# Splitting two of seven key tiles of the attention scores into hi and lo products, with the split made on ScalarE and GpSimd

## What is computed

```python
def _L0_xattn_ref(query, ref, Wq, bq, Wk, bk, Wv, bv):
    Q = query @ Wq + bq
    K = ref @ Wk + bk
    V = ref @ Wv + bv
    scores = jnp.einsum('bqh,bkh->bqk', Q, K)
    attn = jax.nn.softmax(scores, axis=-1) * norm_fact
    return jnp.einsum('bqk,bkh->bqh', attn, V)

x = x + _L0_xattn_ref(_layernorm(x), ctx_1024, Wq, bq, Wk, bk, Wv, bv)
x = x + _L0_attn_ref(_layernorm(x), ...)
x = x + _L0_ffn_ref(_layernorm(x), ...)
```

## Time and profile before

| | before |
|---|---|
| time, median of 3 runs | 238.4 us (237.71 to 238.56) |
| time of the profiled execution | 238.81 us |
| its span, first to last instruction | 237.0 us |
| TensorE busy (matmuls) | 224.4 us, 95% |
| VectorE, ScalarE busy | 136.1 us, 136.6 us |
| GpSimd busy | 105.0 us, 44% |
| granted TensorE clock, mean | 1.000 |
| loaded from HBM | 52.56 MB |

### The profile page before, as it was taken

The page is one execution under the profiler, slowest core; times in us unless marked ns, Lnnn a source line. Parts: engine busy times, 40 slices in busy tenths (PEclk is TensorE's granted clock), DMA queues, the critical chain, the costliest instruction groups (busy, mean ns, idle before and its releaser), DMA issues.

```text
span 237.0 us, 4100 instructions
## 1 busy us (share of the span) xinstructions
PE 224.4 (95%) x1513; PEld 188.8 (80%) x1513; DVE 136.1 (57%) x321; ACT 136.6 (58%) x252; POOL 105.0 (44%) x64
## 2 busy tenths in 40 slices
PE   7989999999999989789998999999999999999994
PEld 7746777777777767579985889974689999999994
DVE  2237555555555554623877876516144748977784
ACT  5146666655555557326878666726405848766570
POOL 1065566666666667330579960000000536555450
PEclk9999999999999999999999999999999999999999
DMA  6999999999999991799700000000000585980000
GB/s 181 376 426 414 417 417 415 420 417 416 423 416 408 410 421 70 247 431 420 319 0 4 0 0 3 1 0 3 0 0 3 178 314 203 408 314 7 0 3 22
DMA packets 8531, 52.92 MB, mean 223 GB/s; under 512 B 953, under 2 KB 1218, under 8 KB 6466
## 3 DMA queue, kind: packets, MB, share of 16 engines
q1 hardware_dynamic: 8514, 52.69, 55.7%
HBM read 52.56 MB, written 0.13 MB: 222 GB/s over the span
## 4 chain that ended last, share of the span: by engine, by line
PE 82%; DMA 6%; DVE 5%; ACT 2%; issue 1%; SPq 1%; ACTq 0%; DVEq 0%
PE psum L427 37%; PE psum L495 14%; PE psum L724 8%; PE psum L422 7%; DMA late_sb<-in_ctx_T 6%; PE psum L622 3%; PE psum L614 3%; PE psum L418 2%; PE psum L648 2%; PE psum L675 1%; PE psum L557 1%; DVE w_lo L1284 1%; PE psum L572 1%; PE psum L631 1%; PE psum L567 1%
## 5 line engine op out<-in xcount | busy, mean ns | idle before, releaser
L360 POOL TENSOR_TENSOR ctx_lo<-ring,ctx_hi 128x1792 fp32r<-128x1792 f32 x13 | 52.4, 4034 | 40.3 <-ACT ctx_hi L788 40.3
L410 POOL TENSOR_TENSOR h_lo<-ring,h_hi 128x512 fp32r<-128x512 f32 x16 | 24.8, 1548 | 66.6 <-ACT h_hi L963 60.6
L427 PE MATMUL psum<-late_sb,work 128*128 128x448 f32 x112 | 44.7, 542 | 1.4 <-DMA late_sb<-in_ctx_T 1.4
L427 PEld LDWEIGHTS psum<-late_sb,work 128*128 128x128 f32 x112 | 20.2, 190 | 18.2 <-issue 17.7
L795 ACT ACTIVATE probsT_hi<-psum 128x512 fp32r<-128x512 f32 (+1 forms) x28 | 13.7, 541 | 32.0 <-PE psum L422 32.0
L1023 DVE TENSOR_REDUCE smalls<-psum 128x1 f32<-128x896 f32 x14 | 15.3, 1091 | 23.3 <-PE psum L427 23.3
L427 PE MATMUL psum<-xT,late_sb 128*128 128x128 f32 x224 | 26.2, 276 | 0.1
L427 PEld LDWEIGHTS psum<-xT,late_sb 128*128 128x128 f32 x224 | 25.5, 192 | 0.3 <-DVE xT L1254 0.3
L788 ACT ACTIVATE ctx_hi<-ring 128x1792 fp32r<-128x1792 f32 x13 | 22.1, 1698 | 2.9 <-DMA ring<-in_ctx 2.9
L495 PE MATMUL psum<-ctx_hi,probsT_hi 128*128 128x256 f32 x98 | 20.6, 327 | 2.5 <-DVE probsT_lo L1047 2.5
L1047 DVE TENSOR_TENSOR probsT_lo<-psum,probsT_hi 128x512 fp32r<-128x512 f32 (+1 forms) x28 | 16.2, 619 | 7.4 <-ACT probsT_hi L795 7.4
(11 more groups left out here) (230 smaller groups left out, 415.0 us busy)
## 6 DMA issues: line engine op xcount, KB each, us to landing
late_sb<-in_ctx_T SPq DMA_DIRECT2D x14, 896.0 KB, 13.7
ring<-in_ctx SPq DMA_DIRECT2D x14, 896.0 KB, 12.2
late_sb<-in_late SPq DMA_DIRECT2D x10, 825.0 KB, 12.1
late_sb<-in_experts SPq DMA_DIRECT2D x8, 1024.0 KB, 6.1
late_slots<-in_experts SPq DMA_DIRECT2D x8, 1024.0 KB, 7.8
early_sb<-in_early SPq DMA_DIRECT2D x1, 512.0 KB, 3.6
early_sb<-in_early SPq DMA_DIRECT2D x1, 465.0 KB, 17.7
work<-in_levels SPq DMA_DIRECT2D x1, 416.0 KB, 19.4
```

The lines of the kernel that those rows point to most:

```text
L360: nc.gpsimd.tensor_tensor(ctxNv[1][:, r % 2], ring[:, r], ctxNv[0][:, r % 2], ALU.subtract).then_inc(s["ctx_lo"], 1)
L410: nc.gpsimd.tensor_tensor(hT[1][:, e % 2, at, :], h32[:, at, :], hT[0][:, e % 2, at, :], ALU.subtract).then_inc(s["h_lo_done"], 1)
L427: last = nc.tensor.matmul(o, lhs(c), rhs(c), start=(c == 0), stop=(c == n - 1))
```

## The change

The scores of groups 3 to 13 are no longer wholly fp32. Of a group's seven key tiles the first two (SPLIT = 256 columns) are computed as three fp32r products: G_hi x T_hi, G_lo x T_hi and G_hi x T_lo, two chunks each, six matmuls of 256 columns. The other five tiles stay fp32, as 448 columns in one bank and 192 in the other.

G_hi is made once by ScalarE and G_lo once by VectorE. T_hi (a 128x512 rounding of the transposed context) is made for each group by ScalarE, ahead of the probs_hi copies, and T_lo (a 128x512 subtraction) by GpSimd. Both are double-buffered. These tiles lie where the last five parts of the late weights go, so these five loads now wait for the last scores. TensorE's part of the loop is unrolled.

```diff
         E_sb = sb("early_sb", EARLY_N)
+        with ExitStack() as overlay:
+            overlay.enter_context(nc.sbuf_tensor("first_parts", [P, FIRST_PARTS * PART_N], F32))
+            T_parts = [overlay.enter_context(nc.sbuf_tensor(f"ctxT_{part}", [P, 2 * DC * SPLIT], F32R)) for part in ("hi", "lo")]
+            G_parts = [overlay.enter_context(nc.sbuf_tensor(f"G_{part}", [P, D], F32R)) for part in ("hi", "lo")]
         W_sb = sb("late_sb", LATE_N + W_SLOTS * EXPERT_N)
...
+            sp.wait_ge(s["scores_ready"], NG)
             for i in range(FIRST_PARTS, LATE_PARTS):
                 part(i, "late2_in")
-            sp.wait_ge(s["scores_ready"], NG)
...
+            def ctxT_lo_parts(g, r):
+
+                pool.wait_ge(s["T_hi"], g - 2)
+                nc.gpsimd.tensor_tensor(Tv[1][:, r % 2], ringT[:, r, :, 0:SPLIT], Tv[0][:, r % 2], ALU.subtract).then_inc(s["T_lo"], 1)
+
+            ctx_lo_parts(0, 0)
+            ctx_lo_parts(1, 1)
+            with pool.Fori(0, 2) as i:
                 for j in range(RING):
-                    ctx_lo_parts(i * RING + j, j)
...
+                    ctx_lo_parts(i * RING + (j + 2), (j + 2) % RING)
+                    ctxT_lo_parts(i * RING + (j + 3), (j + 3) % RING)
+            for g in range(2 * RING, NG - 3):
+                ctx_lo_parts(g + 2, (g + 2) % RING)
+                ctxT_lo_parts(g + 3, (g + 3) % RING)
...
-                for hf in range(2):
-                    last = wide(bank[2 * (r % 2) + hf][:, 0:HALF], lambda c: G[:, c * P:(c + 1) * P],
-                                lambda c: ringT[:, r, c, hf * HALF:(hf + 1) * HALF])
+                b = 2 * (r % 2)
+                last = wide(bank[b + 1][:, 0:HALF], lambda c: G[:, c * P:(c + 1) * P], lambda c: ringT[:, r, c, HALF:GK])
+                plain = SPLIT if split else 0
+                last = wide(bank[b][:, plain:HALF], lambda c: G[:, c * P:(c + 1) * P], lambda c: ringT[:, r, c, plain:HALF])
+                if split:
+                    pe.wait_ge(s["T_hi"], g - 2)
+                    terms = [(u, v, c) for u, v in ((0, 0), (1, 0), (0, 1)) for c in range(DC)]
+                    for i, (u, v, c) in enumerate(terms):
+                        if i == 2 * DC:
+                            pe.wait_ge(s["T_lo"], g - 2)
+                        last = nc.tensor.matmul(bank[b][:, 0:SPLIT], half(G_parts[u], c), Tv[v][:, r % 2, c, :],
+                                                start=(i == 0), stop=(i == len(terms) - 1))
...
-            with pe.Fori(0, 2) as i:
-                for j in range(RING):
-                    r = (j + 2) % RING
-                    scores(i * RING + (j + 2), r, i * 16 + (32 if j >= 2 else 16))
-                    attend(i * RING + j, j)
-                    probs_transposes(i * RING + (j + 1))
-            for g in range(2 * RING, NG - 3):
+            scores(2, 2, 16, split=False)
+            attend(0, 0)
+            probs_transposes(1)
+            pe.wait_ge(s["g_done"], 4)
+            for g in range(1, NG - 3):
                 scores(g + 2, (g + 2) % RING, 16 * ((g + 2) // RING + 1))
                 attend(g, g % RING)
                 probs_transposes(g + 1)
...
+            def ctxT_hi_parts(g, r, filled):
+
+                act.wait_ge(ctxT_in[r], filled)
+                act.wait_ge(s["scores_ready"], g - 1)
+                nc.scalar.activation(Tv[0][:, r % 2], ringT[:, r, :, 0:SPLIT], ACT.Copy).then_inc(s["T_hi"], 1)
+
             with act.Fori(0, 2) as i:
                 for j in range(RING):
                     exps(i * RING + (j + 1), (j + 1) % RING)
+                    ctxT_hi_parts(i * RING + (j + 3), (j + 3) % RING, i * 16 + (32 if j >= 1 else 16))
                     probs_hi_parts(i * RING + (j + 1))
```

More of the change, by code:

```diff
@@ L15 @@
 HALF = GK // 2
+SPLIT = 2 * P
 HK, HV = 4, 8
@@ L144, in perceiver @@
         ctxNv = [part[:, :].rearrange("p (b t d) -> p b t d", b=2, d=D) for part in ctxN]
+        Tv = [part[:, :].rearrange("p (b c k) -> p b c k", b=2, c=DC) for part in T_parts]
         probsT = [part[:, :].rearrange("p (t q) -> p t q", q=T) for part in PT]
@@ L200, in perceiver @@
             late2_in wqk_in dve_chain act_chain pool_chain conv_v y_free mx_done l_done out_ready x_ident aq_done al_low al_middle al_high kn_done xc_done
-            var_done ln_sd ln_xn ln_T ln_xT q_ready q_done q_done_dve g_ready g_done g_done_act qb_ready qb_done bv_ready
-            ctx_hi ctx_lo last_hi last_lo probsT_hi scores_ready max_ready exp_done alpha_done probs_transposed probsT_lo pv_done acc_done
+            var_done ln_sd ln_xn ln_T ln_xT q_ready q_done q_done_dve g_ready g_done qb_ready qb_done bv_ready
+            T_hi T_lo ctx_hi ctx_lo last_parts probsT_hi scores_ready max_ready exp_done alpha_done probs_transposed probsT_lo pv_done acc_done
             o_T o_copied att_ready
@@ L360, in ctx_lo_parts @@
                 nc.gpsimd.tensor_tensor(ctxNv[1][:, r % 2], ring[:, r], ctxNv[0][:, r % 2], ALU.subtract).then_inc(s["ctx_lo"], 1)
-            with pool.Fori(0, 3) as i:
-                for j in range(RING):
-                    ctx_lo_parts(i * RING + j, j)
-            for g in range(3 * RING, NG - 1):
-                ctx_lo_parts(g, g % RING)
+            def ctxT_lo_parts(g, r):
[4 more added lines that the diff above has]
+            with pool.Fori(0, 2) as i:
+                for j in range(RING):
+                    ctx_lo_parts(i * RING + (j + 2), (j + 2) % RING)
[3 more added lines that the diff above has]
+                ctxT_lo_parts(g + 3, (g + 3) % RING)
             g, at = NG - 1, slice(0, 4)
@@ L464, in _, with scores @@
             nc.tensor.matmul(bank[3][:, 0:D], sixteenth[:, :], bv_sb[:, :], start=True, stop=True).then_inc(s["bv_ready"], 1)
-            def scores(g, r, filled, first=False):
+            def scores(g, r, filled, first=False, split=True):
                 if not first:
@@ L493, in attend @@
                         if last_group:
-                            pe.wait_ge(s["last_lo"], 1)
+                            pe.wait_ge(s["last_parts"], 2)
                     last = nc.tensor.matmul(bank[6 + r % 2][:, 0:D], probsT[a][:, t, :], ctxNv[b][:, r % 2, t, :],
@@ L497, in attend @@
                 last.then_inc(s["pv_done"], 1)
-            pe.wait_ge(s["g_done"], 1)
-            pe.wait_ge(s["g_done_act"], 1)
-            scores(0, 0, 16, first=True)
+            pe.wait_ge(s["g_done"], 2)
+            scores(0, 0, 16, first=True, split=False)
             pe.wait_ge(s["qb_done"], 2)
-            scores(1, 1, 16, first=True)
+            scores(1, 1, 16, first=True, split=False)
             probs_transposes(0, first=True)
-            with pe.Fori(0, 2) as i:
-                for j in range(RING):
-                    r = (j + 2) % RING
-                    scores(i * RING + (j + 2), r, i * 16 + (32 if j >= 2 else 16))
-                    attend(i * RING + j, j)
-                    probs_transposes(i * RING + (j + 1))
-            for g in range(2 * RING, NG - 3):
+            scores(2, 2, 16, split=False)
[3 more added lines that the diff above has]
+            for g in range(1, NG - 3):
                 scores(g + 2, (g + 2) % RING, 16 * ((g + 2) // RING + 1))
@@ L768, in _ @@
             act.wait_ge(s["g_ready"], 1)
[L769 removed]
+            nc.scalar.activation(G[:, 0:P], bank[6][:, 0:P], ACT.Copy).then_inc(s["g_done"], 1)
             def exps(g, r, first=False):
@@ L801, in _ @@
             ctx_hi_parts(1, 1, 16, first=True)
+            act.wait_ge(s["g_done"], 2)
+            nc.scalar.activation(G_parts[0][:, :], G, ACT.Copy).then_inc(s["g_done"], 1)
+            def ctxT_hi_parts(g, r, filled):
+                act.wait_ge(ctxT_in[r], filled)
+                act.wait_ge(s["scores_ready"], g - 1)
+                nc.scalar.activation(Tv[0][:, r % 2], ringT[:, r, :, 0:SPLIT], ACT.Copy).then_inc(s["T_hi"], 1)
             with act.Fori(0, 2) as i:
@@ L808, in _ @@
                 exps(g + 1, (g + 1) % RING)
+                ctxT_hi_parts(g + 3, (g + 3) % RING, 16 * ((g + 3) // RING + 1))
                 probs_hi_parts(g + 1)
@@ L1053, in _ @@
             probs_lo_parts(0)
+            dve.wait_ge(s["g_done"], 3)
+            V.tensor_tensor(G_parts[1][:, :], G, G_parts[0][:, :], ALU.subtract).then_inc(s["g_done"], 1)
             with dve.Fori(0, 2) as i:
@@ L1071, in _ @@
             dve.wait_ge(s["pv_done"], g - 1)
-            V.tensor_copy(ctxNv[0][:, g % 2, at], ring[:, g % RING, at]).then_inc(s["last_hi"], 1)
+            V.tensor_copy(ctxNv[0][:, g % 2, at], ring[:, g % RING, at]).then_inc(s["last_parts"], 1)
             maxima(g, g % RING)
             accumulate(g - 1, (g - 1) % 2)
-            dve.wait_ge(s["last_hi"], 1)
-            V.tensor_tensor(ctxNv[1][:, g % 2, at], ring[:, g % RING, at], ctxNv[0][:, g % 2, at], ALU.subtract).then_inc(s["last_lo"], 1)
+            dve.wait_ge(s["last_parts"], 1)
```

(1 more changed line is left out.)

## The result

| | before | after |
|---|---|---|
| time, median | 238.32 us | **312.29 us** (310.98 to 313.35) |
| ratio to before | | 1.3106 (95% interval 1.3048 to 1.3164) |
| profiled execution, span | 238.81, 237.0 us | 312.66, 310.7 us |
| mean granted TensorE clock | 1.000 | 0.889 |

The kernel is 74 us slower. The forecast was 306 us, the range 288 to 320.

A forecast was written before the change was run, and what follows sets the result against it. TensorE, busy 95% of the span and 82% of the chain, was taken to bound the kernel. 238.8 + 50.8 (queue chain) + 0.3 (group 13) = 289.9 us; +16 for the clock gives 306 us, range 288 to 320.

The forecast's parts named there:

- Part 1: TensorE's split score blocks: 2.88 us against 3.01, 0.13 us less each, 1.4 us in all over eleven blocks.
- Part 2: ScalarE's T_hi: a 0.63 us copy once a step, hidden in 2.55 us of idle time; copies of G cost nothing.
- Part 3: GpSimd's T_lo behind ctx_lo closes a chain inside one step: 11.37 us against 6.29, 289.9 us at full clock.
- Part 4: TensorE's clock falls in each 5.2 us wait: 1.6 us a step, bounds 0 to 3.4, +16 us, giving 306.
- all of the path at the low clock: Rival, 13%: in the loop TensorE's clock isn't back before the transposes are done, 3.4 us a step, 324 us.
- no cost: Rival, 20%: the queue chain holds, but TensorE's clock stays or is back before T_lo arrives, 289.9 us.
- Part 5: Five late weight loads wait for the last scores; 10 us of loading, first read over 60 us later: costs nothing.
- The rival on the other side: Rival, 4%: no new chain on GpSimd, T_lo in hand by TensorE's fifth product; only 1.4 us gained, 237.4 us.
- the signs given ahead: Profile after: steps of 11 to 14.5 us, ten TensorE waits of about 5, GpSimd-led chain, PEclk below 9 in loop.

The follow-up runs named there:

- last version: The change with T_lo ahead of ctx_lo, 448 product columns (T_lo's second chunk on VectorE), group 13 fp32, G_hi and G_lo made right after G: 236.10 us.
- bank versions: The change with T_lo ahead of ctx_lo and 448 product columns; G_lo on VectorE 238.45 us, or on GpSimd with group 13 fp32 237.06 us.
- 38-dummy run: The change with 38 dummy 64x64 matmuls on TensorE between its fourth product and the wait for T_lo: 295.27 us, ratio 1.2379.
- first bank version: The change with T_lo ahead of ctx_lo, 448 instead of 256 columns as products, T_lo's second chunk on VectorE: 238.45 us, ratio 0.9976.

## Why the prediction was right, point by point

**Part 1, TensorE's own work: right.** 0.15 us a block (6.13 against 6.29) where 0.13 was worked out. In the change it was worth nothing, as said.

**Part 2, ScalarE: right, with one price wrong off the path.** T_hi takes 0.63 us and is hidden; the run without T_lo loses nothing to it. But of G_lo I said "at most some 0.6 us". It took 4.07 us:

```profile
19.82 4.04 POOL L366 TENSOR_TENSOR ctx_lo<-ring,ctx_hi 128x1792 fp32r<-128x1792 f32 x1 [2.92 <-ACT ctx_hi L809]
...
20.08 4.07 DVE L1086 TENSOR_TENSOR G_lo<-work,G_hi 128x256 fp32r<-128x256 f32 x1 [0.44 <-ACT G_hi L824]
```

It began while GpSimd was in ctx_lo of group 1, which ended at 23.86; G_lo ended at 24.15. VectorE reads two SBUF tiles in it, as in L1284 of the earlier trace rows. I had used the Trainium skill's rule ("SBUF — State Buffer", section "Who interferes with whom") for GpSimd's price and not for VectorE's, where it was the larger by far: 4.07 us, where the same subtraction takes 0.42 in the last version, at 10.08 us, with GpSimd idle. In the change it cost nothing, since TensorE reached its first split block at 24.20 us, when G_lo was just done. In the bank versions G_lo came 2 us late, on VectorE as on GpSimd, until it was made early.

**Part 3, the queue: right, with some luck in the last digit.** The step at full clock was forecast at 11.37 us; the 38-dummy run has 11.41. ctx_lo took 3.97 us for the 4.04, T_lo 1.26 for the 1.30, the hand-over to TensorE 0.04 for the 0.14, together some 0.25 us less than forecast; the two products took 0.50 after a wait at full clock, for the 0.24 of the sum, which is as much more. The errors cancel. The wait was 5.0 us for the forecast 5.2. Group 13 waited too, for the eleventh of the eleven waits. By its own terms 289.9 us, by experiment 291.4.

**Part 4, the clock: the mechanism right, the size too small.** This is the term that was off: "I take 1.6 a step", where the step lost 13.64 - 11.41 = 2.2 us. The range from 0 to 3.4 held it. Two things went into the 1.6: a restart like the program's first, 3.7 us at half speed, and a wish to stay near the middle. The rows show 5.3 us of work on the path at the low clock, that is all of attend (4.48 us for 2.51) and the products (0.80 for 0.50), 2.27 us more than at full clock. Only the transposes were fast again. Ten steps of 0.6 us more are the 6 us between 306 and 312. The Trainium skill's "TensorE: Matmul & The Clock Gate", section "HAM oscillation — how this bites in real kernels", describes a restart at the low clock in every iteration, and the trace agrees, with the clock at 0.50 to 0.52 over each of the ten attentions. Between the two rivals that kept the queue, the truth lay nearer to "all of the path at the low clock" (324 us) than to "no cost" (289.9).

**Part 5, the late weights: right.** Ratio 1.0006 for the move alone.

**The rival on the other side** named its one deciding point, whether T_lo runs ahead of ctx_lo or behind it, and gave 237.4 us for the first. With that order the kernel takes 237.0.

Of the signs given ahead, all came but two: T_lo and T_hi took 1.26 and 0.63 us, the wait on L371 was there eleven times, the stages after the loop were as long as before. The digits of PEclk, as low as 5, weren't below 9 all through the loop: each slice is longer than a low stretch, and a few came out at 9. And the chain isn't "led by GpSimd" on the page, because the tracing found no releaser for much of the loop; the steps in which it did show 5.2 of 13.6 us on GpSimd.

## What to carry to other kernels

Ask of every operation that is added to an idle engine what stands ahead of it in that engine's queue, and what that one waits for. If it is something that the consumer's previous round releases, a chain over two rounds has become a chain in one, however much idle time the engine has. Put the operation that is ready early ahead of the one that is released late. A wait of a few microseconds in every round of a TensorE loop can cost more than its own length: here the clock added 21 us to the chain's 53, since it was low when the work came.

## What the runs showed that I had not expected

- The fall of the clock isn't all or nothing, and it needn't come in the wait. With 2.5 us of idle time in a step, six of ten steps were long (12.9 us) and four were not (11.4), in one execution of one program. In the long ones the clock fell only after TensorE had started again. With 0.4 us none was long, with 5.0 us every one.
- The cost per step doesn't go with the length of the wait: 1.7 us for waits of 2.8 us (10.9 against 9.2; some 1.5 in eight steps, 2.7 in two), 2.2 us for waits of 5.0. It goes with how much of the work behind the wait the low stretch covers.
- Within the change's loop the steps differed by little (13.55 to 13.74 us), and the low stretch lay over the attention in each of them. Whether step and clock hold each other there wasn't tried.
- A VectorE subtraction with two SBUF inputs took 4.07 us for 256 columns beside a GpSimd one, and 0.42 with GpSimd idle. In the loop of the first bank version the one of 448 columns took 2.3 to 2.4 us in nine of eleven steps, and 0.62 in the first.
